# Seven score banks in a ring, one output bank, maxima bank by bank, and more score units prefilled with their maxima

## The reference

```
q, k, v = proj(Wq), proj(Wk), proj(Wv)             # (2, 8, 1024, 64)
dots = einsum('bhqd,bhkd->bhqk', q, k) * scale      # scale = 64 ** -0.5
attn = softmax(dots, axis=-1)
out  = einsum('bhqk,bhkd->bhqd', attn, v)
out  = einsum('bne,ce->bnc', out, Wo) + x
```

## Time and profile before

| | |
|---|---|
| median of 3 runs | 406.17 us (402.18 to 406.69) |
| the profiled execution's own time | 406.31 us |
| its span, first to last instruction | 404.5 us |
| granted TensorE clock, mean | 0.998 |
| one step (159.08 to 196.76 us) | 37.68 us |
| six steps in a row (83.76 to 309.50 us) | 225.74 us |

### The profile page before, as it was taken

One profiled execution on the slowest core, in us unless ns is written; L12 is line 12 of the kernel. 1 busy time (PEld: TensorE's weight loads), 2 busy tenths in 40 slices (PEclk: granted clock), 3 DMA queues, 4 the chain that ended last, 5 costly groups with the idle time before them and its releaser, 6 DMA issues.

```text
span 404.5 us, 6435 instructions
## 1 busy us (share of the span) xinstructions
PE 394.9 (98%) x2486; PEld 236.4 (58%) x2486; DVE 226.7 (56%) x309; ACT 254.5 (63%) x347; POOL 292.9 (72%) x145
## 2 busy tenths in 40 slices
PE   8999999999999999999999999999999989999996
PEld 6865545555464555545545554455458445489995
DVE  5699765565657566655646565566562800664322
ACT  2457666676858576765766675757672696436763
POOL 3071099969899989989998999899999487800021
PEclk9999999999999999999999999999999999999999
DMA  4000101101210121022112312240124015000001
GB/s 146 2 1 1 53 1 54 53 2 53 55 52 2 54 55 52 1 83 40 38 32 76 86 72 55 54 156 2 56 54 158 0 55 156 0 2 15 13 28 52
DMA packets 28226, 19.43 MB, mean 48 GB/s; under 512 B 21248, under 2 KB 23680, under 8 KB 28196
## 3 DMA queue, kind: packets, MB, share of 16 engines
q1 hardware_dynamic: 27620, 18.05, 16.1%
q10 hardware_dynamic: 576, 0.98, 0.7%
HBM read 17.72 MB, written 1.17 MB: 47 GB/s over the span
## 4 chain that ended last, share of the span: by engine, by line
PE 91%; DVE 5%; ACT 2%; issue 1%; ACTq 0%
PE acc_o L600 29%; PE slot L588 26%; PE slot L526 10%; PE slot L514 5%; PE slot L535 4%; PE acc_o L656 4%; PE slot L645 4%; PE acc_o L490 2%; PE slot L465 2%; PE slot L611 2%; DVE half_maxes L990 1%; PE slot L551 1%; PE slot L553 1%; PE acc_o L664 1%; PE slot L439 1%; PE slot L624 1%
## 5 line engine op out<-in xcount | busy, mean ns | idle before, releaser
L990 DVE TENSOR_REDUCE half_maxes<-slot 128x2 f32<-128x1024 f32 x128 | 156.3, 1225 | 96.4 <-PE slot L526 96.2
L778 ACT ACTIVATE probs<-slot 128x1024 f32<-128x1024 f32 x128 | 124.6, 1023 | 82.0 <-PE slot L588 82.0
L600 PE MATMUL acc_o<-probs,v_all 128*64 128x512 f32 x512 | 123.7, 605 | 0.0
L1189 POOL TENSOR_TENSOR sums<-sums,probs 128x1024 f32<-128x1024 f32 x31 | 73.9, 2385 | 2.4 <-ACT probs L778 2.4
L1189 POOL TENSOR_TENSOR odd_sum<-odd_sum,probs 128x1024 f32<-128x1024 f32 x31 | 74.4, 2400 | 0.0
L1189 POOL TENSOR_TENSOR sums<-probs 128x1024 f32<-128x1024 f32 x16 | 37.9, 2369 | 42.4 <-ACT probs L778 42.4
L600 PEld LDWEIGHTS acc_o<-probs,v_all 128*64 128x64 f32 x512 | 31.2, 136 | 58.8 <-issue 39.7
L526 PE MATMUL slot<-k_round,q_round 64*128 64x512 f32 x256 | 56.8, 446 | 1.7 <-DVE half_maxes L990 1.4
L526 PEld LDWEIGHTS slot<-k_round,q_round 64*128 64x128 f32 x256 | 23.6, 183 | 57.2 <-issue 46.3
L588 PE MATMUL slot<-q_round,k_round 64*128 64x512 f32 x256 | 51.6, 399 | 1.1 <-DVE k_rest L985 0.6
L588 PE MATMUL slot<-q_round,k_rest 64*128 64x512 f32 x256 | 50.5, 389 | 0.0
(11 more groups left out here) (123 smaller groups left out, 424.7 us busy)
## 6 DMA issues: line engine op xcount, KB each, us to landing
max_plane<-rows_scratch SPq DMA_DIRECT2D x16, 512.0 KB, 3.7
inv_sb<-inv_scratch SPq DMA_DIRECT2D x14, 256.0 KB, 3.9
max_rows_of<-maxes SPq DMA_DIRECT2D x128, 0.5 KB, 2.0
v_all<-in_fc SPq DMA_DIRECT2D x4, 512.0 KB, 5.6
fc_late<-in_fc SPq DMA_DIRECT2D x4, 512.0 KB, 5.3
out_h<-probs SPq DMA_DIRECT2D x8, 128.0 KB, 1.8
v_all<-in_w ACTq DMA_DIRECT2D x3, 256.0 KB, 3.6
woT<-in_wo SPq DMA_DIRECT2D x1, 256.0 KB, 3.3
```

The costliest lines, as they stand in the source:

```text
L600: last = pe.matmul(acc_o[head_rows(h), cols], v_all[:, s, kc, head_rows(h)], probs[unit(s, kc, half) % TILES][:, h, :], start=(kc == 0), s ...
L778: act.activation(probs[u % TILES][:, :, :].rearrange("p h n -> p (h n)"), slot[:, :], ACT.Exp, scale=SCALE).then_inc(exped, 1)
L990: dve.reduce_max(half_maxes[:, :, qc, keys], slot[:, :].rearrange("p (h n) -> p h n", h=2), AX.X).then_inc(maxed, 1)
L1189: pool.tensor_tensor(chain[:, :, :], first[:, :, :], probs[kc][:, :, :], ALU.add).then_inc(own, 1)
```

## The change

- PSUM becomes one tensor of eight banks. Seven form a ring; the item of turn t takes banks 2t and 2t+1 modulo 7 (`pair_of`), the eighth is the output bank `out_bank`, one for both halves.
- An item's two banks are let go by two different items (`holders`): its first bank by the second bank of the item four turns before, its second bank by the first bank of the item three turns before.
- A `max` item is reduced by two instructions, one per bank, and lets its banks go one after the other.
- When the pair is (6, 0), an exponential, a fill, or a rounding and splitting is two instructions of 512 columns. That is so in each of the steps 1 to 6 for A2, B5, A7 and for k, and in step 0 for B5 and A7.
- The first fill of a step's second half is added (A4), and the units B2, B3, B5, B6, B7 are filled too (`HALVED`): one bank by ScalarE, the other, which a `max` item held, by VectorE (`fill_half`). So 12 of 16 units a step are filled in steps 0 to 6 (11 in step 0), and A1, B1, A3 and A4 in the last step, 87 of 128 in all.
- AHEAD goes from 12 to 14: two more `max` items in the prologue, none left for part 1 of the last step.
- The last step's first output half is copied out by ScalarE, its reciprocal is made in PSUM; the query of token ids at the start is a matmul over 128 rows in place of 8, for which VectorE clears 128 x 512 first.

```diff
-AHEAD = 12
+AHEAD = 14
-PREFILLED = (2, 4, 6)
+PREFILLED, SHARED = (2, 4, 6), (3, 5, 7)
...
-    if part % 4 < 3:
-        items.append(("fill", *units_of(s, part + 1)[0]))
+    if part + 1 < PARTS:
+        items += [("fill", *units_of(s, part + 1)[0]), ("share", *units_of(s, part + 1)[1])]
...
+RING = 7
+def pair_of(turn):
+
+    return (2 * turn % RING, (2 * turn + 1) % RING)
...
+PAIRS_OF = [(2 * (n % SLOTS), 2 * (n % SLOTS) + 1) for n in range(len(PROLOGUE))]
+PAIRS_OF += [pair_of(n) for n in range(len(ALL_ITEMS) - len(PROLOGUE))]
...
+def holders(n):
+
+    found = []
+    for bank in PAIRS_OF[n]:
+        held = [m for m in range(n) if bank in PAIRS_OF[m]]
+        if held:
+            found.append((held[-1], PAIRS_OF[held[-1]].index(bank)))
+    return found
...
+    if item[2] in PREFILLED or item[2:] == (0, 1):
+        return all(kind in WHOLE_SLOT for kind in before)
+    return item[2] in SHARED and before == ["exp", "max"]
+HALVED = [u for u in FILLED if u[1] in SHARED]
...
-                return maxed, MAXES.index(item[1:]) + 1
+                return maxed, 2 * MAXES.index(item[1:]) + 1 + k
...
-                if kc == 0 and s > 0:
-                    pe.wait_ge(o_copied, 2 * s - 1 + half)
+                if kc == 0 and s + half > 0:
+                    pe.wait_ge(o_copied, 2 * s + half)
...
                     if item[0] == "exp" and item[1:] in FILLED:
                         pe.wait_ge(filled_in, FILLED.index(item[1:]) + 1)
+                        if item[1:] in HALVED:
+                            pe.wait_ge(half_filled, HALVED.index(item[1:]) + 1)
                     else:
-                        pe.wait_ge(*release(ALL_ITEMS[n - SLOTS]))
+                        for m, k in holders(n):
+                            pe.wait_ge(*release(ALL_ITEMS[m], k))
...
-                    act.activation(probs[u % TILES][:, :, :].rearrange("p h n -> p (h n)"), slot[:, :],
-                                   ACT.Exp, scale=SCALE).then_inc(exped, 1)
+                    for heads, source in parts_of(PAIRS_OF[n]):
+                        last = act.activation(probs[u % TILES][:, heads, :], source, ACT.Exp, scale=SCALE)
+                    last.then_inc(exped, 1)
...
-                act.wait_ge(*release(ALL_ITEMS[n - SLOTS]))
                 act.wait_ge(plane_loaded, 16 * (2 * s + half) + 16)
-                act.activation(slots[n % SLOTS][:, :], max_planes[half][:, :], ACT.Copy, scale=-1.0).then_inc(filled_in, 1)
+                if unit_item[1:] in HALVED:
+                    own = at_bank(n, 0)
+                    act.wait_ge(*release(ALL_ITEMS[holders(n)[0][0]]))
+                    act.activation(to[:, own, :], plane[:, own, :], ACT.Copy, scale=-1.0).then_inc(filled_in, 1)
+                else:
+                    for m, k in holders(n):
+                        act.wait_ge(*release(ALL_ITEMS[m], k))
...
+            def fill_half(unit_item):
+
+                _, s, kc, half = unit_item
+                n = ALL_ITEMS.index(("exp", s, kc, half))
+                own, plane = at_bank(n, 1), max_planes[half][:, :].rearrange("p (h n) -> p h n", h=2)
+                dve.wait_ge(*release(ALL_ITEMS[holders(n)[1][0]], 0))
+                dve.wait_ge(plane_loaded, 16 * (2 * s + half) + 16)
+                dve.tensor_scalar(pair_view(PAIRS_OF[n])[:, own, :], plane[:, own, :], -1.0, None, ALU.mult).then_inc(half_filled, 1)
```

184 lines of the change are left out of this document (114 added, 70 removed).

## The result

The kernel after takes 409.14 us (median of 4, 409.10 to 410.15) beside 405.92 for the kernel before in the same comparison: ratio 1.0106, 95% interval 1.0062 to 1.015. It is 1.1% slower; 405.2 was forecast, and 1% slower or more had a chance of 0.12.

A forecast was written before the change was run, and what follows sets the result against it. TensorE was taken to bound the kernel, with ScalarE's closed circle 2% behind. Prologue +2.9, middle steps -2.5, step 0 -0.6 and last step -0.6 gave -0.8 to -1.0, so 405.2 us, range 401.3 to 409.2.

The forecast's parts named there:

- The circle: Closed chain in filled parts: fill of A, A's products, exponentials of A and B, next fill; needs about 4.07 us.
- the slack of 0.08: In filled parts lasting 4.15 us, TensorE hides only 0.08 to 0.09 us of ScalarE's closed chain.
- The middle steps: Steps 1 to 6: 0.68 us saved less 0.14 and 0.12, so 0.42 a step, 2.5 in six.
- Pieces: Instructions split at banks 6 and 0: 0.05 us more on ScalarE, 0.06 on VectorE; k 0.12.
- pieces cost their full durations: Rival for split instructions: without overlap in ScalarE's queue each adds 0.15 us, k 0.29; 409.0 us, chance 0.12.
- VectorE's share: Half fills behind both reductions end in time for TensorE in a part: cost nothing.
- the last step: Step 7: A1 comes 0.34 us earlier, ScalarE's own chain gives 0.30; 0.6 won, A4 and A7 cancel.
- one us of slack: In a part VectorE's half fill ends at 3.8 us, TensorE wants it at 4.07 + 0.70.
- The prologue: AHEAD 14: A0 waits for max 14's reduction, k starts at 47.3 us; +2.9 us, bounds 0 and 3.5.
- 2.9 - 0.6: AHEAD 14 costs 2.9 us at the start; step 0, without denominators or split k before its part 1, wins 0.6.
- The start: Clearing the token ids at the very start lies beside other work: 0, at most 0.3 us.
- The sum of -0.8: All terms against the profiled execution: +2.9 - 2.5 - 0.6 - 0.6, given as -0.8 to -1.0 us.

The follow-up runs named there:

- the order is mended: Kernel after with ScalarE's waits ahead of a fill and TensorE's two bank waits put in another order, the later-satisfied one first: 406.18 us, ratio 1.0009.
- the short filler: Kernel after with 8 and 3 small matmuls where TensorE stands still, ahead of max item 15 and of A0: 408.18 us.
- VectorE's half of A: Kernel after with both wait orders changed, VectorE filling half of A ahead of its second reduction, ScalarE the other half and all of B: 399.44 us, ratio 0.9854.
- two experiments: Kernel after with 12 max items in the prologue: 438.93 us; that with both wait orders changed and the last step's B1 not written ahead: 436.29 us.
- one kernel's ten runs: Kernel after with B1 of the last step not written ahead: 407.51 us, ratio 1.0058.

## Why the prediction was wrong, point by point

**The circle** was right, and so was the slack of 0.08, though not its length in the kernel after: parts 5 to 6 and 6 to 7 were to show 4.07 to 4.12 and show 4.20 and 4.23, and 4.12 and 4.15 once the order is mended. Its length can now be put together for each part of the kernel after: 4.07, 0.08 for the late wait, 0.05 for an exponential in two pieces (A2, B5), 0.09 for a fill in two (A2, A7). That gives 4.15 for 4 to 5, 4.20 for 2 to 3 and 5 to 6, 4.24 for 1 to 2 and 6 to 7; measured 4.14, 4.20, 4.20, 4.24, 4.23.

**The middle steps** are where the largest part of the loss against the forecast lies: -0.42 a step forecast, +0.14 measured, and the order of waits is 0.52 of it, 3.1 us in six steps. The step that failed is the sentence that the fill of the next A "still stands behind the exponential of this part's B and still waits for it", taken at the old distance. The list of instructions printed ahead of the prediction shows "[waits plane_loaded,exped]" before and "[waits exped,plane_loaded]" after, and I passed over it. So the prediction's circle of 4.07 had to be 4.15 before any piece was added, and the products saved in the parts that the circle closes had nothing left to win. With the order mended, term by term: part 2 to 3 -0.03 (forecast -0.04 with its piece), 3 to 4 with 4 to 5 -0.25 (-0.23), 5 to 6 -0.02 (0), 6 to 7 +0.01 (-0.04), 7 to 0 -0.22 (-0.23), 1 to 2 +0.01 (0), k +0.12 (+0.12).

**Pieces**: an exponential in two costs 0.05 (start of A2's to start of B2's, 0.97 for 0.93) and k 0.13, as forecast; a fill in two lasts 1.12 for 1.03, so 0.09 and not 0.05, and A2's is not where slack is left. The Trainium skill (Perfetto Trace Analysis, Optimizing Scalar/DVE Operations) gives some 51 ns for a further ScalarE instruction on PSUM and some 93 ns on SBUF: the exponential, which reads PSUM, agrees with the first, and the fill, which reads SBUF and writes PSUM, shows 0.09. The rival "pieces cost their full durations" named 409.0 and the time came out there, but by other causes; k alone would have had to cost 0.29.

**VectorE's share** at no cost was right in the middle steps (with no B written ahead, filled parts keep their length) and wrong at one place. In the last step -0.6 was forecast and +1.68 measured: I followed `max` and square roots there, and not what stands ahead of a half fill in VectorE's queue. The one us of slack that the prediction worked out for a middle part was taken for every part; at this one TensorE waits 1.65.

**The prologue** had the right mechanism: A0's wait was forecast at 3.5, and against the run that has the change's start alone A0 comes 3.67 later (41.13 for 37.46). For prologue and step 0 together 2.9 - 0.6 = 2.3 was forecast, and against the same run step 1 starts 4.2 later (79.90 for 75.68). With the short filler, where the clock behind the prologue stays at 1.00, it is 3.1 (78.76). So 1.1 of what was missed is the lowered clock, for which the prediction had no term; the other 0.8 lies in prologue and step 0, where I have not taken it apart. The first k, forecast 3.05 later, comes 4.57 later (44.85 for 40.28), and 3.2 later in the run with VectorE's half of A, whose clock stayed at 1.00 (43.49). That A4's fill rests on AHEAD 14 I had not seen; it changes nothing in the sum, but it is why two experiments came out some 26 to 36 us above what I expected.

**The start** "0, at most 0.3" was wrong by most: 3.95 in the profiled pair, 3.1 in the medians. The step that failed is that the cleared ids "lie beside other work": the work was weighed, and the clock of TensorE had no term, which is at 1.00 from 4.10 us on and not from 13.37. The size is partly luck, for the profiled execution of before is one with the late start, and some runs have the early one anyhow. Without this gain the kernel after would be some 1.9% slower (an estimate, 1.0106 / 0.9922). The sum of -0.8 thus missed by errors of both signs: -4.0 here, +3.4 in steps 1 to 6 (+0.87 for -2.5; 3.1 of it the order of waits), +2.3 in the last step, +1.9 in prologue and step 0 together (+4.2 for 2.9 - 0.6; 1.1 of it the lowered clock); -0.8 + 3.6 is the +2.8 that was measured.

## What to carry to other kernels

Where an engine's next instruction is on the critical circle, look at which of its waits is attached to it: the one that comes last belongs there. Work handed to an engine with time to spare costs what stands ahead of it in that engine's queue at the one place where it is needed, so read every place and not the average. And when a saved instruction brings nothing, find the closed chain that hides it and shorten that: with the waits in order, the same fills dealt out otherwise gave 1.5% where the change had lost 1.1%, and with a shorter prologue 2.5%. Up to 0.8% of either is TensorE's earlier clock at the start, an estimate from the run that has the 128 rows alone.

## What the runs showed of the hardware

- A wait in an instruction of its own: ScalarE starts 0.031 us behind the end of the instruction that it waits for if that wait is attached, 0.091 if it stands ahead in an instruction of its own, 0.113 if two waits do.
- TensorE's granted clock fell to 0.50 (1.2 GHz) behind some 3 us in which it had almost nothing to do, in the kernel after and several of its variants, and stayed at 1.00 in one with the same stand-still. Part 0 of step 0 took 1.0 to 1.8 us longer with it (7.79 and 8.63 for 6.80); of one kernel's ten runs those at a mean granted clock of 0.994 to 0.996 took 1.2 to 1.9 us more than those at 1.000, those at 0.990 2.3 to 2.6. 22 small matmul records in the gap kept it at 1.00.
- At the start TensorE ran 128x128 matmuls 0.213 us apart until the trace's first record of the granted clock (13.37 us in the profiled execution of before) and 0.112 behind it. The engines' table prints 1.00 on both sides, since ahead of the first record it has no entry:

```profile
8.00:10.00 2.00, 2.00 (x11) 2.00 (x11) 1.04 (x2) 0.00 (x0) 0.00 (x0) 1.00 0.43 156
```

```profile
8.00:10.00 2.00, 2.00 (x20) 2.00 (x19) 1.14 (x9) 1.10 (x2) 0.00 (x0) 1.00 0.45 148
```

The first is the kernel before, whose records begin at 13.37, the second the same with 128 rows, whose records begin at 5.79: 11 and 20 matmuls in the same 2 us. From 14 to 16 us the kernel before has 20 too:

```profile
14.00:16.00 2.00, 2.00 (x20) 2.00 (x19) 1.25 (x10) 0.89 (x3) 0.00 (x0) 1.00 0.00 0
```

So read the distance of equal matmuls beside the granted clock when the stretch lies ahead of the first record.
